# One-hot columns and six tiles of rows of a routing table, built by comparisons with a scalar per partition

## The chip, the cores and the metric

The kernel runs on one core of a Trainium2 chip. The metric is the device time of one execution in microseconds (us), from the first to the last instruction with what lies around them. Three runs of the kernel before gave 1054.81 us as their median (1053.97 to 1056.63).

## What is computed

Two residual blocks follow one another on `x` (8 x 256 tokens of 512 numbers): a cross attention, and a mixture of experts. Only the second matters here:

```python
logits = x2d @ gate_w.T                       # 2048 tokens, 32 experts
rw = softmax(logits)
_, sel = top_k(sigmoid(logits), 4)            # 4 experts per token
w = take_along_axis(rw, sel); w = w / w.sum(-1)
large = sum over e of (silu(x @ Wg[e]) * (x @ Wu[e]) * cw_large[:, e]) @ Wd[e]      # 192 wide
small = the same with 16 shared experts, expert e // 2                               # 128 wide
x = x + large + 0.05 * small
```

The 2048 tokens give 8192 pairs of a token and an expert. The kernel sorts the pairs by expert into slots of 128 rows and computes one expert in each slot.

## The kernel before

There are three stages: `attention`, `route` and `experts`. Each is a block in which the five engines run their own programs and meet at its end.

**Attention** takes about the first 390 us and is not touched.

**Route** (L991 on) works on 16 tiles (`NT`) of 128 tokens, in 4 groups of 4 (`GT`). TensorE makes the logits. VectorE takes the four largest (`largest`), and its `rows(g)` works out the place of each pair within its expert. The low seven bits of the place are the row within a slot; their negative is kept in `rf`, an fp32 tensor with one value for each token of a tile and each of the `K_` = 4 choices. The rest of the place and the first slot of the expert give the slot, `qf`, an fp32 tensor of the same shape. There are `NS` = 96 possible slots.

The table of tokens by row and slot is then a sum of 64 products on TensorE (L1302), four to a tile: a 128 x 128 fp16 matrix `rown[:, t, k, :]`, which in each partition (a token) holds the token's number in the column of its row and 0 elsewhere, times a 128 x 96 fp16 matrix `ohq[:, t, k, :]`, which holds 1 in the column of its slot. For each tile TensorE waits for `rown` (`rown_ready`) and for `ohq` (`ohq_ready`).

`rown` is made in two ways. For tiles 0 to 9 (`COMPARED` = 10) ScalarE makes it alone, in its own `rows(g)`: four activations (L1165) take the distance |iota + rf| into `away`, and a fifth (L1168) turns it into number * relu(1 - distance). For tiles 10 to 15 VectorE compares first: one `tensor_tensor` for a tile (L1413) compares `iota_n` (0, -1, -2, ...; fp16, repeated over the 4 choices by a stride of 0) with `rf` (repeated over the 128 columns) into `ohr`, 4 x 128 fp16 elements to a partition; ScalarE then multiplies it by the token's number (`numbers(t)`, L1149) after its last `rows` and after it has issued the store of the weights (L1204).

VectorE's order in this part is its own program's: `rows(2)`, `rows(3)`, ten small instructions (L1401 to L1410), the six comparisons of `ohr` (L1413), a wait for TensorE's `base_full` (the product at L1295, which waits for ScalarE's last `oh_evac`, L1154), `qf` (L1416), then sixteen comparisons of `ohq` (L1418), one for a tile with 4 x 96 fp16 elements to a partition, then a wait for TensorE's `tab_full` and five instructions (L1422 to L1427) that turn the table into `tok` and `dst`, the lists by which the experts gather and add rows. With `dst` the block ends.

**Experts** (L1430 on) begins when all engines have left the route block. GpSimd gathers 128 rows by `tok` (L1501, L1504), VectorE turns them (L1599), a chain of small transfers issued by ScalarE turns them further (L1545, `xT`), and TensorE computes gate and up (L1636), a transpose (L1645) and down (L1653), for 78 slots one after the other.

Of the kernel before, what the change touches and what calls it, by code (L numbers as in the profile page):

```python
# [5 lines left out]
ALU = mybir.AluOpType  # L6
ACT = mybir.ActivationFunctionType
# [5 lines left out]
F16 = mybir.dt.float16  # L13

P = 128
# [4 lines left out]
NT = NB * TT  # L20
# [942 lines left out]
E_, K_ = 32, 4  # L963
TILE = P
NS = (NT * P * K_) // TILE + E_
# [10 lines left out]
COMPARED = 10  # L976
# [14 lines left out]
def route(nc, gw, gw_loaded, xs, ident, new, xd, out, tabs, wts, W, w_loaded, kept, xd_stored):  # L991
# [5 lines left out]
    with ExitStack() as ctx:  # L997
        sb = lambda n, s, d: ctx.enter_context(nc.sbuf_tensor(n, s, d))
        ps = lambda n, s: ctx.enter_context(nc.psum_tensor(n, s, F32))
        sem = lambda n: ctx.enter_context(nc.semaphore(n))  # L1000
# [20 lines left out]
        iota_r = sb("iota_r", [P, P], F16)  # L1021
        iota_q = sb("iota_q", [P, NS], F16)
        iota_n = sb("iota_n", [P, P], F16)
        ohr = sb("ohr", [P, NT - COMPARED, K_, P], F16)
        none = sb("none", [P, 1], F32)
        number, minus = sb("number", [P, NT], F32), sb("minus", [P, NT], F32)
        away = [sb(f"away{i}", [P, K_, P], F16) for i in range(2)]
# [10 lines left out]
        rf, jf, qf = (sb(n, [P, NT, K_], F32) for n in ("rf", "jf", "qf"))  # L1038
# [5 lines left out]
        rown = sb("rown", [P, NT, K_, P], F16)  # L1044
        ohq = sb("ohq", [P, NT, K_, NS], F16)
# [9 lines left out]
        step = sem("r_step")  # L1055
        var_ready, ln_ready, root_ready, late_ready = sem("r_var"), sem("r_ln_ready"), sem("r_root"), sem("late_ready")
        zeros_ready, zeros_stored, w_ready, w_stored = sem("zeros_ready"), sem("zeros_stored"), sem("w_ready"), sem("w_stored")
        ohr_ready = sem("ohr_ready")
        id4_ready, ohq_ready = sem("id4_ready"), sem("ohq_ready")
        oh_ready, ohT_full, ohT_ready, bsel_ready, base_full = (sem(n) for n in (  # L1060
            "oh_ready", "ohT_full", "ohT_ready", "bsel_ready", "base_full"))
        minus_ready, rf_ready, away_ready, rown_ready = (sem(n) for n in ("minus_ready", "rf_ready", "away_ready",
                                                                         "rown_ready"))
# [8 lines left out]
        def of(g):  # L1072

            return slice(g * GT, (g + 1) * GT)
# [5 lines left out]
        @block.sync  # L1080
        def _(sp):
            for n in range(2):
                load_piece(sp, wts, W, w_loaded, 0, 0, n)
            for t in range(LATE, NT):
                sp.wait_ge(late_ready, t - LATE + 1)
                sp.dma_start(xd[t * P:(t + 1) * P, 0:D], xl[:, t - LATE, :]).then_inc(xd_stored, DMA)
            sp.wait_ge(zeros_ready, 1)
            sp.dma_start(out[NT * P:(NT + 1) * P, :], zeros[:, :]).then_inc(zeros_stored, DMA)
            for p in range(1, NW):
                for n in range(2):  # L1090
                    load_piece(sp, wts, W, w_loaded, 0, p, n)
            for p in range(2):
                sp.wait_ge(kept[p], NT // 2 * DMA)
            sp.wait_ge(xd_stored, NT * DMA)
            sp.wait_ge(zeros_stored, DMA)
            sp.wait_ge(w_stored, DMA)
# [30 lines left out]
        @block.scalar  # L1127
        def _(act):
            def x_evac(t):
                act.wait_ge(xt_full, t + 1)  # L1130
                if t // GT >= 2:
                    act.wait_ge(part_full, t // GT - 1)
                act.copy(xnT[t // GT % 2][:, :, t % GT * P:(t % GT + 1) * P],
                         xt_ps[t % 2][:, :].rearrange("p (c t) -> p c t", c=C)).then_inc(xt_empty, 1)

            def parts_evac(g):
                act.wait_ge(part_full, g + 1)
                if g >= 2:
                    act.wait_ge(lg_full, g - 1)
                act.copy(parts[g % 2][:, :], part_ps[g % 2][:, :]).then_inc(part_ready, 1)  # L1140

            def lg_evac(g):
                act.wait_ge(lg_full, g + 1)
                act.copy(lg[:, of(g), :], lg_ps[:, of(g), :]).then_inc(lg_ready, 1)

            def numbers(t):

                act.wait_ge(ohr_ready, t - COMPARED + 1)
                act.activation(rown[:, t, :, :], ohr[:, t - COMPARED, :, :], ACT.Copy,  # L1149
                               scale=number[:, t:t + 1]).then_inc(rown_ready, 1)  # L1150

            def oh_evac(g):
                act.wait_ge(ohT_full, g + 1)
                act.copy(ohT[:, of(g), :], xt_ps[g % 2][:, :].rearrange("p (t n) -> p t n", t=GT)).then_inc(ohT_ready, 1)  # L1154

            def exponentials(g):
                act.wait_ge(d4_ready, g + 1)
                act.activation(e4[:, of(g), :], d4[:, of(g), :], ACT.Exp).then_inc(e4_ready, 1)

            def rows(g):  # L1160

                act.wait_ge(rf_ready, g + 1)
                for t in range(g * GT, min((g + 1) * GT, COMPARED)):
                    for k in range(K_):
                        m = act.activation(away[t % 2][:, k, :], iota_r[:, :], ACT.Abs, bias=rf[:, t, k:k + 1])  # L1165
                    m.then_inc(away_ready, 1)
                    act.wait_ge(away_ready, t + 1)
                    act.activation(rown[:, t, :, :], away[t % 2][:, :, :], ACT.Relu, bias=number[:, t:t + 1],  # L1168
                                   scale=minus[:, t:t + 1]).then_inc(rown_ready, 1)

            act.preload_act_table_set("natural_log_exp_and_others")
            x_evac(0)
            x_evac(1)
            act.wait_ge(var_ready, 1)
            act.activation(ln[:, LATE:NT], mv[:, LATE:NT, 1], ACT.Ln, bias=eps[:, :]).then_inc(ln_ready, 1)
            act.wait_ge(ln_ready, 1)
            act.activation(root[:, LATE:NT], ln[:, LATE:NT], ACT.Exp, scale=-0.5).then_inc(root_ready, 1)
            for t in range(2, GT + 2):
                x_evac(t)
            for g in range(NG - 1):  # L1180
                parts_evac(g)
                x_evac((g + 1) * GT + 2)
                lg_evac(g)
                x_evac((g + 1) * GT + 3)
                if g < NG - 2:
                    x_evac((g + 2) * GT)
                    x_evac((g + 2) * GT + 1)
                    exponentials(g)
            parts_evac(NG - 1)
            lg_evac(NG - 1)  # L1190
            exponentials(NG - 2)
            act.wait_ge(minus_ready, 1)
            act.wait_ge(iotas, 2)
            oh_evac(0)
            rows(0)
            oh_evac(1)
            oh_evac(2)
            exponentials(NG - 1)
            rows(1)
            oh_evac(NG - 1)  # L1200
            rows(2)

            act.wait_ge(w_ready, NG)
            act.dma_start(xd[:, D:D + E_].rearrange("(t p) e -> p t e", p=P), wrow[:, :, :]).then_inc(w_stored, DMA)  # L1204
            for t in range(COMPARED, NT):
                numbers(t)

        @block.tensor
        def _(pe):
# [84 lines left out]
            for t in range(NT):  # L1294
                m = pe.matmul(lg_ps[:, t, 0:K_], ohT[:, t, :], bsel[:, :], start=True, stop=True)  # L1295
            m.then_inc(base_full, 1)

            for t in range(NT):
                pe.wait_ge(rown_ready, t + 1)
                pe.wait_ge(ohq_ready, t + 1)  # L1300
                for k in range(K_):
                    m = pe.matmul(tab_ps[:, 0:NS], rown[:, t, k, :], ohq[:, t, k, :], start=(t == 0 and k == 0),  # L1302
                                  stop=(t == NT - 1 and k == K_ - 1))
# [3 lines left out]
        def _(dve):  # L1307
# [102 lines left out]
            dve.tensor_scalar(slot_buf[:, 0:NS], slot_e[:, 0:NS], NW - 1, None, ALU.bitwise_and)  # L1410

            for t in range(COMPARED, NT):
                dve.tensor_tensor(ohr[:, t - COMPARED, :, :], iota_n[:, :].unsqueeze(1).broadcast_to([P, K_, P]),  # L1413
                                  rf[:, t, :].unsqueeze(2).broadcast_to([P, K_, P]), ALU.is_equal).then_inc(ohr_ready, 1)
            dve.wait_ge(base_full, 1)
            done(dve.tensor_tensor(qf[:, :, :], lg_ps[:, :, 0:K_], jf[:, :, :], ALU.add))  # L1416
            for t in range(NT):
                dve.tensor_tensor(ohq[:, t, :, :], iota_q[:, :].unsqueeze(1).broadcast_to([P, K_, NS]),  # L1418
                                  qf[:, t, :].unsqueeze(2).broadcast_to([P, K_, NS]), ALU.is_equal).then_inc(ohq_ready, 1)

            dve.wait_ge(tab_full, 1)
            done(dve.tensor_copy(tabf[:, :], tab_ps[:, 0:NS]))  # L1422
# [317 lines left out]
```

## Time and profile before

| | |
|---|---|
| median of three runs | 1054.81 us |
| the profiled execution: its own time | 1054.6 us |
| its span | 1052.9 us |
| TensorE busy | 983.6 us (93%) |
| VectorE busy | 524.5 us (50%) |
| ScalarE busy | 314.0 us (30%) |
| mean granted TensorE clock | 0.968 of full speed |

PE is TensorE's matmuls and PEld its weight loads, DVE is VectorE, ACT ScalarE, POOL GpSimd, SP SyncE. "L1418" is line 1418 of the kernel. Times are us from the first instruction, means of one instruction are in ns. "idle before" is the time that an engine stood still ahead of the instructions of a group, and "<-" names what it waited for. An instruction's duration is longer than the interval from its start to the start of the next on the same engine, because independent instructions overlap.

### The profile page before, as it was taken

How to read it: one execution, taken by the hardware profiler on the slowest of the kernel's cores; microseconds unless marked ns; L12 is line 12 of the kernel's file. 1: busy time of each engine (PE TensorE's matmuls, PEld its weight loads, DVE VectorE, ACT ScalarE, POOL GpSimd, SP SyncE). 2: the span in 40 equal slices, each digit the busy share in tenths (PEclk: the TensorE clock that was granted, in tenths of full speed). 3: DMA queues.
4: the chain of work that ended last, by engine and by line, in shares of the span. 5: the costliest groups of instructions: out<-in, count | busy, mean ns of one | idle time of the engine just before them, and what ended most of it. 6: DMA issues, size and time to landing. Idle time of an engine off the chain costs nothing.

```text
span 1052.9 us, 18703 instructions
## 1 busy us (share of the span) xinstructions
PE 983.6 (93%) x5163; PEld 723.9 (69%) x5164; DVE 524.5 (50%) x1233; ACT 314.0 (30%) x631; POOL 300.2 (29%) x399
## 2 busy tenths in 40 slices
PE   8789999999999987449999999999999999999994
PEld 6556667676665545337787777878777787877872
DVE  5677677777677727923333333333333333333331
ACT  2245465555555536801111111111111111111110
POOL 3012101011120002223443434344343443434432
PEclk9999999999999999569999999999999999999997
DMA  6153234331431019138888998989888899889563
GB/s 215 44 163 77 75 84 102 87 87 58 121 80 51 32 41 354 47 83 201 217 219 199 253 252 213 259 206 256 201 224 213 207 259 244 214 207 252 113 112 71
DMA packets 102603, 168.23 MB, mean 160 GB/s; under 512 B 15520, under 2 KB 65824, under 8 KB 98208
## 3 DMA queue, kind: packets, MB, share of 16 engines
q1 hardware_dynamic: 36624, 103.11, 31.3%
q0 software_dynamic: 17792, 43.30, 22.6%
q10 hardware_dynamic: 48144, 21.25, 7.3%
q8 instruction: 27, 0.44, 0.2%
q14 instruction: 16, 0.13, 0.0%
HBM read 101.29 MB, written 29.36 MB: 124 GB/s over the span
## 4 chain that ended last, share of the span: by engine, by line
PE 55%; DMA 1%; issue 1%; DVEq 0%; DVE 0%; ACTq 0%; POOL 0%; ACT 0%; POOLq 0%
PE y_ps L1653 19%; PE g_ps L1636 17%; PE u_ps L1636 16%; PE at_ps L1645 2%; DMA xg<-xd,gidx 0%; DMA xT<-xb 0%; ACTq L1545 0%; POOL out_x L1518 0%; DVEq L1621 0%; DVE xb L1599 0%; ACT sg L1550 0%; DVEq L1586 0%; ACT yb L1556 0%; DVE aT L1582 0%; DVEq L1622 0%
## 5 line engine op out<-in xcount | busy, mean ns | idle before, releaser
L1653 PE MATMUL y_ps<-W,aT 128*128 x468 | 216.2, 598 | 3.6 <-DVE aT L1582 3.6
L1518 POOL DMA_INDIRECT out_x<-yb,yidx x78 | 125.3, 1606 | 278.4 <-ACT yb L1556 159.7
L1636 PE MATMUL g_ps<-W,xT 128*128 x624 | 192.5, 452 | 12.8 <-DMA xT<-xb 12.8
L519 DVE TENSOR_REDUCE mx<-s 128x2 f32<-128x512 f32 x256 | 163.6, 682 | 59.4 <-PE s L710 58.6
L398 ACT ACTIVATE pt<-stp 128x512 f32<-128x512 f32 x256 | 139.1, 596 | 146.6 <-PE stp L724 145.9
L1636 PE MATMUL u_ps<-W,xT 128*128 x624 | 180.7, 432 | 0.0
L1636 PEld LDWEIGHTS g_ps<-W,xT 128*128 128x128 f32 x624 | 168.3, 311 | 15.2 <-issue 15.1
L1636 PEld LDWEIGHTS u_ps<-W,xT 128*128 128x128 f32 x624 | 171.0, 308 | 0.1
L1653 PEld LDWEIGHTS y_ps<-W,aT 128*128 128x128 f32 x468 | 89.6, 192 | 85.7 <-issue 79.6
L1599 DVE STREAM_TRANSPOSE xb<-xg 128x512 f32<-128x512 f32 x80 | 89.1, 1114 | 102.6 <-DMA xg<-xd,gidx 99.8
L1550 ACT ACTIVATE sg<-g_ps 128x320 f32<-128x320 f32 x78 | 34.2, 438 | 302.4 <-PE u_ps L1636 302.4
L1603 DVE SCALAR_TENSOR_TENSOR a<-u_ps,wt,sg 128x192 f32<-128x192 f32 x78 | 32.6, 418 | 160.8 <-ACT sg L1550 158.9
L1556 ACT COPY yb<-y_ps 128x512 f32<-128x512 f32 x78 | 45.7, 585 | 201.2 <-DMA out_x<-yb,yidx 125.4
L1504 POOL DMA_INDIRECT xg<-xd,gidx x82 | 82.7, 1008 | 65.4 <-POOL gidx L1501 64.7
L710 PE MATMUL s<-kst,qst 96*128 96x256 bf16 x512 | 81.6, 274 | 10.8 <-DVE mx L519 9.9
L1582 DVE COPY aT<-at_ps 128x384 f32<-128x384 f32 x78 | 43.5, 558 | 86.8 <-PE at_ps L1645 81.9
L724 PE MATMUL stp<-qst,kst 98*128 98x256 bf16 x512 | 78.5, 276 | 4.2 <-DMA qst<-nm 4.1
L710 PEld LDWEIGHTS s<-kst,qst 96*128 96x128 bf16 x512 | 43.7, 97 | 51.8 <-DVE mx L519 24.5
L740 PE MATMUL ov<-pt,vx 128*32 128x256 f32 x1024 | 70.3, 393 | 2.0 <-ACT xo L382 2.0
L1501 POOL COPY gidx<-tok 128x1 uint32 (+1 forms) x82 | 60.0, 732 | 28.1 <-POOLq L997 17.2
L724 PEld LDWEIGHTS stp<-qst,kst 98*128 98x128 bf16 x512 | 49.4, 98 | 17.7 <-issue 5.7
L1645 PEld LDWEIGHTS at_ps<-ident,a 128*128 128x128 f32 x234 | 30.2, 140 | 43.7 <-issue 42.0
(203 smaller groups left out, 869.5 us busy)
## 6 DMA issues: line engine op xcount, KB each, us to landing
W<-in_wts SPq DMA_DIRECT2D x32, 1280.0 KB
W<-in_wts SPq DMA_DIRECT2D x32, 768.0 KB
xT<-xb ACTq DMA_DIRECT2D x320, 64.0 KB
qst<-q SPq DMA_DIRECT2D x42, 256.0 KB, 5.0
xs<-in_x SPq DMA_DIRECT2D x8, 512.0 KB, 3.7
ctxT<-in_ctx SPq DMA_DIRECT2D x8, 512.0 KB, 4.2
out_x<-xs SPq DMA_DIRECT2D x16, 256.0 KB, 2.3
kst<-k SPq DMA_DIRECT2D x48, 64.0 KB, 2.3
```

Source lines behind the costliest of these rows:

```text
L398: act.activation(pt[g % 2][:, 2 * (j % 2) + r, :, :], stp[n % STP][:, :, :], ACT.Exp, scale=DH ** -0.5).then_inc(exp_done, 1)
L519: dve.tensor_reduce(mx[j // CH % 2][:, h:2 * G:G], s1[r][:, :, :], AX.X, ALU.max)\
L710: m = pe.matmul(s1[r][:, t, :], qst[b % 2][0:ROWS_QK, head(j, r), t * P:(t + 1) * P], kst[b % 2][0:ROWS_QK, head(j, r) // C, :], start=Tru ...
L724: m = pe.matmul(stp[n % STP][:, t, :], kst[b % 2][0:ROWS_ST, head(j, r) // C, t * P:(t + 1) * P], qst[b % 2][0:ROWS_ST, head(j, r), :], st ...
L740: m = pe.matmul(ov[c * VW:(c + 1) * VW, g % 2, :], vx[b % 2][:, t, g % 2 * C + c, :], pt[(b * G + g) % 2][:, c, t, :], start=(t == 0), sto ...
L1501: pool.tensor_copy(idx[p][:, :], tok[:, bass.ds(s, 1)]).then_inc(idx_ready, 1)
L1504: pool.indirect_dma_start(xg[p][:, :], None, xd[:, :], bass.IndirectOffsetOnAxis(idx[p][:, :], 0))\
L1518: pool.indirect_dma_start(out[:, :], bass.IndirectOffsetOnAxis(yidx[p][:, :], 0), yb[p][:, :], None, compute_op=ALU.add).then_inc(y_added, ...
L1599: dve.transpose(xb[p][:, :].rearrange("p (j r c) -> p j c r", r=Q, c=C), xg[p][:, 0:D]).then_inc(turned, 1)
L1636: m = pe.matmul(ps_[p][:, 0:IW], xT[p][:, :, c], W[:, bass.ds(buf, 1), (2 * c + g) * IW:(2 * c + g + 1) * IW] .rearrange("p a f -> p (a f) ...
L1645: m = pe.transpose(at_ps[:, c, :], a[p][:, c * P:(c + 1) * P], ident[:, :])
L1653: m = pe.matmul(y_ps[:, :], aT[p][:, c, :], W[:, bass.ds(buf, 1), GW + c * D:GW + (c + 1) * D].rearrange("p a d -> p (a d)"), start=(c == ...
```

## The change

The six comparisons of `ohr` and ScalarE's six multiplications go. VectorE makes `rown` of tiles 10 to 15 itself, by 24 `tensor_scalar` instructions, four to a tile: each takes 128 columns of `iota_n`, compares with one column of `rf` (a scalar for each partition, read through a pointer) and multiplies by `number` (a second such scalar). The sixteen comparisons of `ohq` become 64 `tensor_scalar` instructions, four to a tile, each of 96 columns of `iota_q` with one such scalar, a column of `qf`. A semaphore is raised by the last instruction of a tile; `late_rows` takes the place of `rown_ready` for tiles 10 to 15. Nothing else is changed; the buffer `ohr` is dropped.

```diff
@@ route @@
-        ohr = sb("ohr", [P, NT - COMPARED, K_, P], F16)
...
-        ohr_ready = sem("ohr_ready")
+        late_rows = sem("late_rows")
@@ ScalarE @@
-            def numbers(t):
-
-                act.wait_ge(ohr_ready, t - COMPARED + 1)
-                act.activation(rown[:, t, :, :], ohr[:, t - COMPARED, :, :], ACT.Copy,
-                               scale=number[:, t:t + 1]).then_inc(rown_ready, 1)
...
-            for t in range(COMPARED, NT):
-                numbers(t)
@@ TensorE @@
             for t in range(NT):
-                pe.wait_ge(rown_ready, t + 1)
+                if t < COMPARED:
+                    pe.wait_ge(rown_ready, t + 1)
+                else:
+                    pe.wait_ge(late_rows, t - COMPARED + 1)
                 pe.wait_ge(ohq_ready, t + 1)
@@ VectorE @@
             for t in range(COMPARED, NT):
-                dve.tensor_tensor(ohr[:, t - COMPARED, :, :], iota_n[:, :].unsqueeze(1).broadcast_to([P, K_, P]),
-                                  rf[:, t, :].unsqueeze(2).broadcast_to([P, K_, P]), ALU.is_equal).then_inc(ohr_ready, 1)
+                for k in range(K_):
+                    m = dve.tensor_scalar(rown[:, t, k, :], iota_n[:, :], rf[:, t, k:k + 1], number[:, t:t + 1],
+                                          ALU.is_equal, ALU.mult)
+                m.then_inc(late_rows, 1)
             dve.wait_ge(base_full, 1)
             done(dve.tensor_tensor(qf[:, :, :], lg_ps[:, :, 0:K_], jf[:, :, :], ALU.add))
             for t in range(NT):
-                dve.tensor_tensor(ohq[:, t, :, :], iota_q[:, :].unsqueeze(1).broadcast_to([P, K_, NS]),
-                                  qf[:, t, :].unsqueeze(2).broadcast_to([P, K_, NS]), ALU.is_equal).then_inc(ohq_ready, 1)
+                for k in range(K_):
+                    m = dve.tensor_scalar(ohq[:, t, k, :], iota_q[:, :], qf[:, t, k:k + 1], None, ALU.is_equal)
+                m.then_inc(ohq_ready, 1)
```

## Rows read from the trace of the kernel before

**Rows 1.** The page: busy tenths in 40 slices of 26.3 us each.

```profile
PE   8789999999999987449999999999999999999994
DVE  5677677777677727923333333333333333333331
PEclk9999999999999999569999999999999999999997
```

**Rows 2.** Chain of work that ended last, 425 to 470: start, us, what.

```profile
448.68 0.19 POOL gidx L1501
...
456.49 2.92 DMA xT<-xb
...
459.66 4.25 PE g_ps L1636 x8
```

**Rows 3.** Busy time by stretch; behind each engine's (x instructions) PEclk, DMA share, GB/s.

```profile
434.80:438.60 3.80, 0.59 (x16) 0.51 (x16) 3.80 (x8) 3.73 (x9) 0.00 (x0) 0.50 0.01 2
438.60:446.90 8.30, 7.51 (x64) 4.70 (x64) 7.63 (x17) 5.75 (x12) 0.00 (x0) 0.50 0.21 34
...
600.00:800.00 200.00, 200.00 (x684) 157.56 (x683) 72.23 (x163) 28.22 (x55) 81.44 (x109) 1.00 0.89 230
```

**Rows 4.** Timeline of the table's making: start, us, engine, line, what.

```profile
434.81 3.69 DVE L1413 TENSOR_TENSOR ohr<-iota_n,rf 128x512 f16<-128x512 f16 x6
436.73 0.59 PE L1295 MATMUL r_lg<-bsel,ohT 128*128 128x4 bf16 x16 [7.75 <-ACT ohT L1154]
438.42 0.22 DVE L1416 TENSOR_TENSOR qf<-r_lg,jf 128x64 f32<-128x64 f32 x1
438.67 7.59 DVE L1418 TENSOR_TENSOR ohq<-iota_q,qf 128x384 f16<-128x384 f16 x16
439.90 0.81 ACT L1168 ACTIVATE rown<-away,number,minus 128x512 f16<-128x512 f16 x1
440.62 3.77 ACT L1149 ACTIVATE rown<-ohr,number 128x512 f16<-128x512 f16 x6
446.38 0.29 PEld L1302 LDWEIGHTS tab_ps<-ohq,rown 128*128 128x128 f16 x4 [0.17 <-issue]
```

**Rows 5.** Timeline of DVE behind the table, 446.8 to 448.9.

```profile
446.92 0.26 DVE L1422 COPY tabf<-tab_ps 128x96 f32<-128x96 f32 x1 [0.66 <-PE tab_ps L1302]
447.22 0.27 DVE L1424 TENSOR_SCALAR empty<-tabf,none 128x96 f32<-128x96 f32 x1
447.52 0.21 DVE L1425 TENSOR_SCALAR tok<-tabf 128x96 uint32<-128x96 f32 x1
```

**Rows 6.** Groups of DVE instructions: xcount | busy us, mean ns | idle before.

```profile
L1413 DVE TENSOR_TENSOR ohr<-iota_n,rf 128x512 f16<-128x512 f16 x6 | 3.7, 684 | 0.0
L1418 DVE TENSOR_TENSOR ohq<-iota_q,qf 128x384 f16<-128x384 f16 x16 | 7.6, 551 | 0.0
L1377 DVE TENSOR_SCALAR iota_n<-iota_r 128x128 f16<-128x128 f16 x1 | 0.2, 188 | 0.0
L1404 DVE TENSOR_SCALAR more<-cum_i 128x1 int32<-128x1 int32 x1 | 0.2, 154 | 0.0
```

**Rows 7.** Timeline of DVE at 399.7, x5 in a row.

```profile
399.70 2.37 DVE L1372 TENSOR_SCALAR xl<-xs,mv_new,rstd_new 128x512 f32<-128x512 f32 x5
401.99 0.17 DVE L1376 TENSOR_SCALAR minus<-number 128x16 f32<-128x16 f32 x1
```

**Rows 8.** Timeline of DVE, 427.2 to 428.7.

```profile
427.48 0.25 DVE L1393 TENSOR_SCALAR bsel<-kmask,basep 128x4 bf16<-128x4 f32 x1
427.65 0.17 DVE L1394 TENSOR_TENSOR end_x<-cum,ident 32x32 f32<-32x32 f32 x1
...
428.06 0.26 DVE L1396 TENSOR_SCALAR past<-iota_s,end 32x96 bf16<-32x96 f32 x1
428.25 0.15 DVE L1341 TENSOR_REDUCE s<-e 128x4 f32<-128x16 f32 x1
```

**Rows 9.** DMA issues, 395 to 475: engine op xcount, KB each, us to landing.

```profile
xd<-wrow ACTq DMA_DIRECT2D x1, 256.0 KB, 3.3
```

## The prediction

> **What bounds the kernel now.** I read the busy tenths first [rows 1]. TensorE is at 9 tenths nearly everywhere, except in two slices at about 421 to 473 us, the route and the start of the experts. VectorE is at 9 tenths in one slice of the whole span, and it is the same one. So a change to VectorE's comparisons in the route can matter there only. Next the chain that ended last [rows 2]: from 448.68 on it is the gather with its index, the turning transfer, and from 459.66 TensorE alone, slot after slot. In the stretch 600 to 800 TensorE is busy 200.00 of 200.00 us [rows 3], so there is no slack behind the route in which a delay could vanish or a gain be lost: a microsecond at 448 is a microsecond at the end.
>
> Third, the stretches ahead of that point [rows 3]. From 434.8 to 438.6 VectorE is busy 3.80 of 3.80 us, with the six comparisons of `ohr`; from 438.6 to 446.9 it is busy 7.63 of 8.30 us, with `qf` and the sixteen comparisons of `ohq`. GpSimd does nothing in either. TensorE's 64 matmuls run beside `ohq`, but they follow it: the last four weight loads start at 446.38, behind the last comparison's end at 438.67 + 7.59 = 446.26 [rows 4], and VectorE waits 0.66 us for their product, until 446.92 [rows 5]. ScalarE's six multiplications of `ohr` run from 440.62 to 444.39 [rows 4], for tiles 10 to 15, whose `ohq` comes later: they lie under VectorE's work. So the end of the route is VectorE's own queue: `ohr`, `qf`, `ohq`, the wait for TensorE, five small instructions. The question is only whether 24 + 64 `tensor_scalar` take less or more of VectorE's time than 6 + 16 `tensor_tensor`.
>
> **What the removed instructions cost.** L1413 takes 684 ns for 512 elements, L1418 551 for 384 [rows 6]. The difference is 133 ns for 128 elements, 1.04 ns for one: one element in a cycle of 0.96 GHz. What counts in a queue of independent instructions is the interval. The six `ohr` take from 434.81 to 438.42, where `qf` starts: 3.61 us, 0.602 each, that is 0.533 for the elements and 0.069 fixed. The sixteen `ohq` take 7.59 us [rows 4], with an interval of (7.59 - 0.55) / 15 = 0.469, 0.400 and again 0.069.
>
> **What an added instruction costs.** No row shows this form in a queue, so I build its price from three parts.
>
> Elements: L1377, 128 fp16 elements with a constant, takes 188 ns, and L1404, one element, 154 [rows 6]. The difference of 34 ns for 127 elements is four in a cycle. For 128 elements that is 33 ns and for 96 it is 25.
>
> Fixed: 0.069 in the interval as above, the same in both kinds of `tensor_tensor`.
>
> The scalar for each partition: L1372 has two of them. Its five run in a row, 2.37 us with the last at 541 ns by this count: the interval to L1376 included it is (401.99 - 399.70) / 5 = 0.458 [rows 7]. Its 512 fp32 elements would take 0.533 at one in a cycle, which is more than the whole, so they go at two, 0.267. With 0.069 fixed, 0.122 is left, 0.061 for each scalar. L1424 and L1425 say the same in durations: both have 96 fp32 elements, L1424 compares, multiplies and has one such scalar, 0.27 against 0.21 [rows 5], 0.06 more. L1424 also shows that a comparison does not fall to one element a cycle, since that alone would be 0.05 more. A larger value stands in L1393, four elements and one scalar: L1394 starts 0.17 behind it [rows 8], so up to 0.10 for the scalar. From L1396 (96 elements, one scalar) to L1341 it is 0.19 [rows 8].
>
> So one added `ohr` instruction: 0.069 + 2 x 0.061 + 0.033 = 0.224. One added `ohq` instruction: 0.069 + 0.061 + 0.025 = 0.155 by this sum, at least 0.17 if L1393's interval is a floor, and at most L1396's 0.19. I take 0.16, nearest the sum, because L1372 is the only row that shows such instructions behind one another.
>
> **A rule beside it.** The row above gives each such instruction an interval of 0.155 us or more. The Trainium skill (VectorE: DVE Perf Modes, The TRN2 errata) has 58 cycles + elements / mode for an instruction from SBUF to SBUF, with no term for a scalar that is read through a pointer: an estimate of 82 cycles, 0.085 us, for 96 fp16 elements at four a cycle. For the removed L1418 it gives 442 cycles, 0.460, and the trace agrees with 0.469. By it the change would gain some 3 us. The same page's rules for kernel authors say to minimize the number of operations, which speaks against 88 in place of 22.
>
> **The sum.**
> - `ohr`: 24 x 0.224 = 5.38 us in place of 3.61: +1.77. `qf` then starts at 440.2. Its operand from TensorE is there at 436.73 + 0.59 = 437.32 [rows 4], so the wait for it costs nothing, as before.
> - `ohq`: 63 x 0.16 + 0.24 for the last one whole = 10.32 us in place of 7.59: +2.73. With 0.155 it is +2.4, with 0.17 +3.4, with 0.19 +4.6.
> - ScalarE's six multiplications, 3.77 us: nothing gained, they were hidden under `ohq`. Its last `rown` of its own, tile 9, comes at 440.71 [rows 4]; `ohq` of tile 9 would be ready at about 440.5 + 10 x 0.64 = 446.9, so TensorE doesn't wait for ScalarE.
> - TensorE: its four matmuls for a tile fit in 0.47 us now [rows 4], and would have 0.64. The 0.66 us behind the last comparison stays.
> - The end of the block: SyncE also waits for the store of the weights, issued at 439.90 (L1204, right ahead of L1149 in ScalarE's queue, so not moved) and landing 3.3 us later [rows 9], about 443.2: hidden.
> - The granted clock is 0.50 through these stretches [rows 3], the lower level of 1.2 GHz, since TensorE does little; it would be so for longer, but TensorE has nothing on the path until 459.66 but four short matmuls.
>
> Together +1.77 + 2.73 = +4.5 us. The profiled execution took 1054.6 us of its own, 0.2 below the median of 1054.81; from the median the forecast is 1059.3 us. Bounds of this case: +4.1 (0.155) to +5.2 (0.17), +6.4 with 0.19.
>
> What a measurement can tell from no change is 0.3%, 3.2 us, here.
>
> **The rivals.**
> 1. *The scalar costs nothing in a queue*, its read lying under the instruction ahead. Then `ohr` takes 24 x 0.102 = 2.45 us and ends at 437.26; `qf` waits until about 437.4 for TensorE: -1.0. `ohq` takes 63 x 0.094 + 0.18 = 6.1: -1.5. Together -2.5: 1052.3 us, on the other side, though within what can be told; the point from which it decides is 0.11 us for an `ohq` instruction, below which the stage becomes shorter if `ohr` is cheap too. The page's formula would be a little beyond it. Against it stands L1372: five in a row, 0.122 us more each than elements and fixed part. 10%.
> 2. *The faster mode isn't had*: with an fp32 scalar the fp16 elements go at two a cycle. `ohr` 24 x 0.257 = 6.18 (+2.57), `ohq` 63 x 0.18 + 0.27 = 11.6 (+4.0): +6.6, 1061.4 us. For it: all rows with a pointer have fp32 elements, so none shows four a cycle. 8%. At one a cycle it would be 24 x 0.324 (+4.2) and 63 x 0.230 + 0.32 (+7.2): 1066.2 us; L1372 and L1424 speak against. 4%.
> 3. *0.10 for each scalar*, as L1393 has it: `ohr` 24 x 0.302 = 7.25 (+3.6), `ohq` 63 x 0.194 + 0.28 = 12.5 (+4.9): +8.5, 1063.3 us. Against it: L1372's two scalars cost 0.122 together, and L1393's scalar had been written by the instruction just ahead. 9%.
> 4. *The delay is taken up further on*, so that the time is the same. Only the start of the experts has room, TensorE's idle time until 459.66, and it begins with the gather, which needs `tok`. 4%.
>
> **How the numbers follow.** The forecast has 65%: 1059.3 us, by its bounds 1058.9 to 1061.2. The range leaves out rivals 1 and 4 and the one-a-cycle case, 18%: 1056.8 to 1063.8 us. Faster by over 0.3% (below 1051.65): the far side of rival 1, 3%. Within 0.3%: the rest of rival 1, rival 4, and a forecast whose `ohq` comes out under 0.14: 16%. Slower by over 0.3%: 81%.
>
> **What the profile after would show.** L1149 gone from ScalarE; 24 instructions into `rown` on VectorE of about 310 ns (0.154 + 0.122 + 0.033), 0.22 apart, and 64 into `ohq` of about 240 ns, 0.16 apart; `qf` at 440.2, the last `ohq` ending at 450.8, `tabf` at 451.4, the first gather's index at 453.2, TensorE's first gate matmul at 464.2, and every slot from there as long as before. Durations near 190 for `ohq` mean rival 1, 265 rival 2, 280 rival 3. The prediction is wrong if the intervals in these two runs of instructions aren't what the sum says, or if the interval between `tabf` and the first gate matmul is not 12.7 us as now.

## The result and the profile after

The changed kernel takes 1058.76 us (median of 22 runs), the kernel before, run beside it, 1054.33 us (22 runs). The ratio is 1.0039, with a 95% interval of 1.0024 to 1.0054: slower by 0.39%, 4.1 us (2.5 to 5.7). The two medians themselves lie 4.4 us apart, well inside that interval. The measured time is inside the range of the prediction and on the side it gave 81%. It fits the forecast of +4.5 us closer than a measurement with this interval can tell, so how near the two came is in part luck.

The timeline of the changed kernel where the table is made (start, us, engine, line, what), to be laid beside [rows 4] and [rows 5]. Line numbers have moved: L1408 writes `rown`, L1415 writes `ohq`, L1419 is `tabf`.

```profile
432.81 5.43 DVE L1408 TENSOR_SCALAR rown<-iota_n,rf,number 128x128 f16<-128x128 f16 x24
434.76 0.59 PE L1286 MATMUL r_lg<-bsel,ohT 128*128 128x4 bf16 x16 [7.76 <-ACT ohT L1147]
437.93 0.81 ACT L1161 ACTIVATE rown<-away,number,minus 128x512 f16<-128x512 f16 x1
438.14 0.24 DVE L1412 TENSOR_TENSOR qf<-r_lg,jf 128x64 f32<-128x64 f32 x1
438.42 2.72 DVE L1415 TENSOR_SCALAR ohq<-iota_q,qf 128x96 f16<-128x96 f16 x17
...
440.89 7.49 DVE L1415 TENSOR_SCALAR ohq<-iota_q,qf 128x96 f16<-128x96 f16 x48
...
449.04 0.26 DVE L1419 COPY tabf<-tab_ps 128x96 f32<-128x96 f32 x1 [0.66 <-PE tab_ps L1296]
```

Two lengths are to be read. From the first late `rown` to `qf` it is 438.14 - 432.81 = 5.33 us, where the six comparisons took 3.61. From the first `ohq` to the end of the last it is 440.89 + 7.49 - 438.42 = 9.96 us, where they took 7.59. Whole, from the first of these instructions to `tabf`: 16.23 us in place of 446.92 - 434.81 = 12.11, +4.12 us, which lies in the interval of the measured difference. ScalarE's L1149 is gone, and the engine has nothing to compute from 438.7 on; that gives nothing back.

The groups of the same stretch (mean ns of one) and TensorE's waits in it:

```profile
L1415 DVE TENSOR_SCALAR ohq<-iota_q,qf 128x96 f16<-128x96 f16 x64 | 10.0, 245 | 0.0
L1296 PE MATMUL tab_ps<-ohq,rown 128*128 128x96 f16 x64 | 7.6, 269 | 6.0 <-DVE ohq L1415 3.9
L1408 DVE TENSOR_SCALAR rown<-iota_n,rf,number 128x128 f16<-128x128 f16 x24 | 5.4, 322 | 0.0
```

VectorE has no idle time ahead of either group. The chain that ended last shows what lies behind:

```profile
450.80 0.20 POOL gidx L1498
...
461.77 4.65 PE g_ps L1633 x8
```

From `tabf` to the first gate matmul it is 461.77 - 449.04 = 12.73 us, and was 459.66 - 446.92 = 12.74. Behind it TensorE is full, as in [rows 3] (busy by stretch: PE, PEld, DVE, ACT, POOL, then the granted clock, DMA share, GB/s):

```profile
600.00:800.00 200.00, 199.98 (x680) 156.48 (x680) 72.65 (x166) 28.10 (x55) 82.41 (x110) 1.00 0.89 231
```

The points in time that the prediction gave (`qf` at 440.2, `tabf` at 451.4) are off by 2.0 us although the lengths are right: this execution reached the stage 2.0 us sooner, 432.81 against 434.81, in work that the change doesn't touch. The span in the profile therefore grew by 2.4 us only, and the medians are what tells the difference. This is taken up in the last section.

### The profile page after: what moved, and what is told of

It reads as the page before. It is cut to its first block, busy times and chain, and to the rows that moved or that the text cites. A ratio compares the mean times of both kernels' runs of the same rounds, so it can differ in the third digit from the quotient of the medians.

```text
span 1055.3 us, 18763 instructions
## 1 busy us (share of the span) xinstructions
PE 981.2 (93%) x5163; PEld 722.5 (68%) x5164; DVE 529.8 (50%) x1299; ACT 310.2 (29%) x625; POOL 300.9 (29%) x399
## 4 chain that ended last, share of the span: by engine, by line
PE 54%; DMA 1%; issue 1%; DVEq 0%; DVE 0%; ACTq 0%; POOL 0%; ACT 0%; SPq 0%; POOLq 0%
PE y_ps L1650 19%; PE g_ps L1633 17%; PE u_ps L1633 16%; PE at_ps L1642 2%; DMA xg<-xd,gidx 0%; DMA xT<-xb 0%; ACTq L1542 0%; POOL out_x L1515 0%; DVEq L1618 0%; DVE xb L1596 0%; ACT sg L1547 0%; DVEq L1583 0%; ACT yb L1553 0%; DVE aT L1579 0%; DVEq L1619 0%
## 5 line engine op out<-in xcount | busy, mean ns | idle before, releaser
L1633 PE MATMUL g_ps<-W,xT 128*128 x624 | 192.6, 452 | 13.0 <-DMA xT<-xb 12.8
```

The source lines that it names most:

```text
L1633: m = pe.matmul(ps_[p][:, 0:IW], xT[p][:, :, c], W[:, bass.ds(buf, 1), (2 * c + g) * IW:(2 * c + g + 1) * IW] .rearrange("p a f -> p (a f) ...
```

## The experiments

**The slots alone.** The kernel before with the edit of `ohq` only.

```diff
             for t in range(NT):
-                dve.tensor_tensor(ohq[:, t, :, :], iota_q[:, :].unsqueeze(1).broadcast_to([P, K_, NS]), ...
+                for k in range(K_):
+                    m = dve.tensor_scalar(ohq[:, t, k, :], iota_q[:, :], qf[:, t, k:k + 1], None, ALU.is_equal)
+                m.then_inc(ohq_ready, 1)
```

> Only the comparisons of ohq by a scalar per partition (64 in place of 16); ohr and ScalarE's multiplications as before. My account: the sixteen tiles of ohq take 9.95 us from the first to the end of the last, in place of 7.59, so +2.4 us in all, 0.2%: from the start of ohr to tabf 14.5 us in place of 12.11. Rival (the slower table lets ScalarE's own work come on the path, or the delay is taken up further on): TensorE waits for rown, or the distance from tabf to the first gate matmul is not 12.7 us.

Measured: ratio 1.0019 (1.0002 to 1.0036), 1057.16 us. The timeline of this run:

```profile
437.62 3.70 DVE L1413 TENSOR_TENSOR ohr<-iota_n,rf 128x512 f16<-128x512 f16 x6
...
441.49 9.96 DVE L1419 TENSOR_SCALAR ohq<-iota_q,qf 128x96 f16<-128x96 f16 x64
443.47 3.77 ACT L1149 ACTIVATE rown<-ohr,number 128x512 f16<-128x512 f16 x6
...
447.25 0.29 PEld L1302 LDWEIGHTS tab_ps<-ohq,rown 128*128 128x128 f16 x4 [0.32 <-ACT rown L1149]
...
452.11 0.26 DVE L1423 COPY tabf<-tab_ps 128x96 f32<-128x96 f32 x1 [0.66 <-PE tab_ps L1302]
```

From the first `ohr` to `tabf` 14.49 us, expected 14.5, +2.4. From `tabf` to the first gate matmul (464.86) 12.75 us. The profile puts six waits of TensorE's weight loads, 1.9 us in all, down to ScalarE's late rows (L1149). That can't be the cause: these waits lie between 443.8 and 447.3, ahead of tiles 3 to 8, which use none of the late rows, and the last of those rows was done at 447.24 (443.47 + 3.77), before tile 10 began. TensorE waited for `ohq`, tile by tile, 0.62 us apart, and `tabf` waits the same 0.66 us. The rival is out.

**The rows alone.** The changed kernel with its `ohq` put back to sixteen `tensor_tensor`, so that only the late rows are by `tensor_scalar`.

```diff
             for t in range(COMPARED, NT):
-                dve.tensor_tensor(ohr[:, t - COMPARED, :, :], iota_n[...], rf[...], ALU.is_equal).then_inc(ohr_ready, 1)
+                for k in range(K_):
+                    m = dve.tensor_scalar(rown[:, t, k, :], iota_n[:, :], rf[:, t, k:k + 1], number[:, t:t + 1],
+                                          ALU.is_equal, ALU.mult)
+                m.then_inc(late_rows, 1)
```

> Only the rows of the last six tiles by VectorE alone (24 in place of 6, no multiplications on ScalarE); ohq as before. My account: the 24 take 5.33 us in place of 3.61, so +1.7 us: 13.85 us from the first of them to tabf. ScalarE's freed 3.77 us give nothing back. Rival (ScalarE's multiplications held TensorE up in the kernel before): less than +1.7, with TensorE's table matmuls ending closer behind the last ohq.

Measured: ratio 1.0005 (0.9991 to 1.0020), 1054.68 us. The time can't tell it from no change, nor from the expected 1.0016. The timeline can:

```profile
436.07 5.44 DVE L1408 TENSOR_SCALAR rown<-iota_n,rf,number 128x128 f16<-128x128 f16 x24
...
441.41 0.23 DVE L1412 TENSOR_TENSOR qf<-r_lg,jf 128x64 f32<-128x64 f32 x1
441.67 7.59 DVE L1414 TENSOR_TENSOR ohq<-iota_q,qf 128x384 f16<-128x384 f16 x16
...
449.92 0.26 DVE L1418 COPY tabf<-tab_ps 128x96 f32<-128x96 f32 x1 [0.66 <-PE tab_ps L1296]
```

It is 13.85 us from the first late row to `tabf`, +1.74. That is the number expected, but the expectation took its 5.33 us from the changed kernel's trace; new is that the halves add up and that ScalarE gives nothing back: `tabf` waits 0.66 us for TensorE as before, so ScalarE's multiplications had not held anything up. The two halves, +2.38 and +1.74, add up to the +4.12 of the whole.

**The price of a scalar.** These lengths fit the prediction's sum, but one alone fits others too: 0.155 us could be 0.069 fixed, 0.061 for the scalar and 96 elements at four a cycle, or the same fixed part, 0.036 for the scalar and elements at two a cycle. By the second reading an instruction of the late rows would take 0.069 + 2 x 0.036 + 0.067 = 0.208 us where 0.222 was measured, which speaks against it, but by 0.014 us and with a fixed part that is itself inferred. So the parts were measured by themselves, in queues of 12 behind the end of the route in the changed kernel.

```diff
             done(dve.tensor_scalar(dst[:, :], far[:, :], 1.0, None, ALU.subtract))
+            for i in range(12):
+                m = dve.tensor_scalar(junk[:, i, 0:NS], iota_q[:, :], 3.0, None, ALU.is_equal)
+            done(m)
+            for i in range(12):
+                m = dve.tensor_scalar(junk[:, i, 0:NS], iota_q[:, :], qf[:, i, 0:1], None, ALU.is_equal)
+            done(m)
...
+            for i in range(12):
+                done(dve.tensor_scalar(fresh[:, i:i + 1], number[:, i:i + 1], 1.0, None, ALU.mult))
+                dve.tensor_scalar(junk[:, i, 0:4], iota_q[:, 0:4], fresh[:, i:i + 1], None, ALU.is_equal)
+                done(dve.tensor_scalar(junk[:, i, 8:12], iota_q[:, 0:4], 3.0, None, ALU.is_equal))
```

> The changed kernel, and behind its last instruction in the route seven queues of 12 independent instructions each on VectorE into buffers that nothing reads: fp16, 96 elements with a constant; with one scalar per partition; with two; 4 elements with one; 96 fp32 elements with one; a tensor_tensor of 384 fp16 elements whose innermost dimension is the four choices, contiguous in all three operands; and a pair in which the scalar has been written by the instruction ahead. My account (0.069 fixed, 0.061 for a scalar, four fp16 elements a cycle, two fp32): intervals 0.094, 0.155, 0.216, 0.131, 0.180, 0.27 us. Rival that the faster mode is lost beside a scalar (two fp16 a cycle, so a scalar costs 0.035): 0.094, 0.155, 0.19, 0.106, 0.155. Rival that a floor of 0.15 to 0.17 stands for any instruction with a scalar, whatever its size: the third and fourth are both near 0.155 to 0.17. The pair: 0.17 from the instruction with the fresh scalar to the next, if L1393's row means that a scalar just written is dearer; 0.131 if it doesn't.

The timeline of that run. The interval is (length - duration of one) / 11, in the last queue the mean from the start of the instruction with the scalar to the start of the next. "One" is the median duration.

```profile
449.95 0.26 DVE L1424 COPY tabf<-tab_ps 128x96 f32<-128x96 f32 x1 [0.66 <-PE tab_ps L1301]
...
451.83 1.22 DVE L1433 TENSOR_SCALAR junk<-iota_q 128x96 f16<-128x96 f16 x12
453.08 1.95 DVE L1436 TENSOR_SCALAR junk<-iota_q,qf 128x96 f16<-128x96 f16 x12
455.06 2.67 DVE L1439 TENSOR_SCALAR junk<-iota_q,qf,number 128x96 f16<-128x96 f16 x12
457.77 1.66 DVE L1442 TENSOR_SCALAR junk<-iota_q,qf 128x4 f16<-128x4 f16 x12
459.46 2.24 DVE L1445 TENSOR_SCALAR junk<-iota_s,qf 128x96 f32<-128x96 f32 x12
461.74 3.31 DVE L1448 TENSOR_TENSOR junk<-iota_qk,q 128x384 f16<-128x384 f16 x12
...
465.28 0.23 DVE L1453 TENSOR_SCALAR junk<-iota_q,fresh 128x4 f16<-128x4 f16 x1
465.41 0.17 DVE L1454 TENSOR_SCALAR junk<-iota_q 128x4 f16<-128x4 f16 x1
...
482.87 4.65 PE L1663 MATMUL g_ps<-W,xT 128*128 x8 [32.96 <-DMA xT<-xb]
```

| queue | one, ns | interval, us | expected |
|---|---|---|---|
| 96 fp16, a constant | 186 | 0.094 | 0.094 |
| 96 fp16, one scalar | 244 | 0.155 | 0.155 |
| 96 fp16, two scalars | 303 | 0.215 | 0.216 |
| 4 fp16, one scalar | 224 | 0.131 | 0.131 |
| 96 fp32, one scalar | 261 | 0.180 | 0.180 |
| 384 fp16, `tensor_tensor`, choices innermost | 354 | 0.269 | 0.27 |
| 4 fp16, the scalar just written | 229 | 0.136 | 0.131 or 0.17 |

Each scalar adds 0.061, the first and the second alike. 92 elements more add 0.024 us beside a scalar, which is four a cycle: the faster mode is kept. And a small instruction with a scalar goes at 0.131, so there is no floor at 0.155 to 0.17. Both rivals are out. A scalar that has just been written costs 0.005 us more at most, so the 0.17 behind L1393 [rows 8] has another cause, which none of these runs shows.

This run also shows how much of a delay in this place arrives at the end: the queues, with two copies ahead of them, take from 451.20 to 471.32, 20.1 us. From `tabf` to the first gate matmul it is 482.87 - 449.95 = 32.92 us, 20.2 more than in the changed kernel. The program ran once, in 1079.17 us, 20.4 more than the changed kernel's median; runs of that kernel lie up to 9 us apart, so this last agreement is worth less than the one in the trace.

**Two a cycle for the `tensor_tensor`.** The queues say that a `tensor_tensor` can have what the change sought, if its operands allow it: fp16 throughout, with the same innermost dimension of step 1, which here are the four choices. The scalars are kept in fp16, GpSimd writes the counting columns four times over at the start, where it is idle, and TensorE and ScalarE read with a stride of four. VectorE then has time to spare and ScalarE has not, so `COMPARED` goes to 8.

```diff
-COMPARED = 10
+COMPARED = 8
...
-        ohr = sb("ohr", [P, NT - COMPARED, K_, P], F16)
+        ohr = sb("ohr", [P, NT - COMPARED, P, K_], F16)
...
-        ohq = sb("ohq", [P, NT, K_, NS], F16)
+        ohq = sb("ohq", [P, NT, NS, K_], F16)
...
-            pool.iota(iota_q[:, :], [[1, NS]], 0, 0, allow_small_or_imprecise_dtypes=True)
+            pool.iota(iota_qk[:, :, :], [[1, NS], [0, K_]], 0, 0, allow_small_or_imprecise_dtypes=True)
+            pool.iota(iota_rk[:, :, :], [[1, P], [0, K_]], 0, 0, allow_small_or_imprecise_dtypes=True)
...
+            dve.tensor_copy(r16[:, COMPARED:NT, :], ri[:, COMPARED:NT, :])
...
-                dve.tensor_tensor(ohq[:, t, :, :], iota_q[:, :].unsqueeze(1).broadcast_to([P, K_, NS]),
-                                  qf[:, t, :].unsqueeze(2).broadcast_to([P, K_, NS]), ALU.is_equal).then_inc(ohq_ready, 1)
+                dve.tensor_tensor(ohq[:, t, :, :], iota_qk[:, :, :],
+                                  q16[:, t:t + 1, :].broadcast_to([P, NS, K_]), ALU.is_equal).then_inc(ohq_ready, 1)
```

> The kernel before with tensor_tensor kept, but fp16 operands whose innermost dimension is the four choices, contiguous in both inputs and the output (the scalars in fp16, the counting columns repeated four times by GpSimd at the start), and COMPARED 8 in place of 10, so that VectorE and ScalarE share the rows otherwise. My account: two elements a cycle in place of one, 0.336 us for a tile of ohr (eight tiles, 2.7 us in place of 3.6) and 0.27 for a tile of ohq (4.3 in place of 7.6); then TensorE's matmuls at the low clock or ScalarE's eight multiplications (until about 441.8 on the clock of the rows of before) end last, tabf at about 443.6 in place of 446.92: -3.3 us. Rival (the stride of 0 in the second input keeps the one element a cycle): no gain, durations 550 and 684 ns as before. Rival (the strided reads by TensorE and ScalarE cost more): TensorE's matmuls longer than 280 ns apiece or ScalarE's multiplication longer than 707.

Measured: ratio 0.9967 (0.9952 to 0.9983), 1050.63 us, faster than both kernels. Its timeline:

```profile
433.15 2.77 DVE L1415 TENSOR_TENSOR ohr<-iota_rk,r 128x512 f16<-128x512 f16 x8
...
434.84 5.30 ACT L1151 ACTIVATE rown<-ohr,number 128x512 f16<-128x512 f16 x8
...
436.09 4.39 DVE L1420 TENSOR_TENSOR ohq<-iota_qk,q 128x384 f16<-128x384 f16 x16
436.60 5.71 PE L1304 MATMUL tab_ps<-ohq,rown 128*128 128x96 f16 x64 [1.01 <-DVE ohq L1420]
442.34 0.26 DVE L1424 COPY tabf<-tab_ps 128x96 f32<-128x96 f32 x1 [1.86 <-PE tab_ps L1304]
```

9.19 us from the first `ohr` to `tabf`, in place of 12.11: -2.9, expected -3.3 by the times in the rows of before (a cast of the rows to fp16, 0.08 us, lies ahead of this length). The stride of 0 sits in the middle dimension now and doesn't keep it from going at two elements a cycle. The fp32 operand and the stride of 0 in the innermost dimension went together here, so which of the two had held it at one a cycle isn't shown. VectorE is done 1.86 us before `tabf`: TensorE ends last, with 64 matmuls in 5.71 us. ScalarE's multiplication takes 759 ns here in place of 707, and 731 in the next run, which reads with the same stride; so the stride is not the whole of it. A TensorE matmul is recorded with 265 ns in place of 280 (medians), but what counts is the interval, which is taken up in the last section.

The same with `COMPARED` left at 10:

> As the run with the four choices innermost, but COMPARED left at 10. My account: VectorE's work shrinks as there (six tiles of ohr 2.1 us, sixteen of ohq 4.4), but ScalarE ends its own rows of tile 9 only 5.9 us behind the first ohr and needs six multiplications of 0.66 us then, so its last rown comes 9.9 us behind the first ohr, and tabf at about 10.5, in place of 9.19 there and 12.11 in the kernel before: about -1.6 us, with TensorE waiting for ScalarE's rown. Rival (ScalarE's multiplications are hidden as in the kernel before, so COMPARED makes no difference): tabf 9.2 us behind the first ohr.

Measured: ratio 0.9978 (0.9960 to 0.9995), 1052.03 us.

```profile
436.83 2.10 DVE L1415 TENSOR_TENSOR ohr<-iota_rk,r 128x512 f16<-128x512 f16 x6
...
439.56 4.39 DVE L1420 TENSOR_TENSOR ohq<-iota_qk,q 128x384 f16<-128x384 f16 x16
...
442.57 3.93 ACT L1151 ACTIVATE rown<-ohr,number 128x512 f16<-128x512 f16 x6
447.11 0.26 DVE L1424 COPY tabf<-tab_ps 128x96 f32<-128x96 f32 x1 [3.16 <-PE tab_ps L1304]
```

10.28 us, expected 10.5. VectorE is as fast as in the run before this one and waits 3.16 us at the end. ScalarE's late rows, free under the slow `ohq`, now end at 446.50 and bound the stage. Work that is hidden in one version is a price in the next.

Last, the operand of `qf` made earlier, and `ohr` and `ohq` in turn, on top of `COMPARED` 8:

```diff
@@ ScalarE, rows(g) @@
                 for t in range(g * GT, min((g + 1) * GT, COMPARED)):
+                    if t == GT + 1:
+                        oh_evac(NG - 1)
...
             rows(1)
-            oh_evac(NG - 1)
-            rows(2)
@@ VectorE @@
-            for t in range(COMPARED, NT):
-                dve.tensor_tensor(ohr[:, t - COMPARED, :, :], iota_rk[:, :, :], ...)
...
+            late = COMPARED
             for t in range(NT):
                 dve.tensor_tensor(ohq[:, t, :, :], ...)
+                if t >= 1 and late < NT:
+                    dve.tensor_tensor(ohr[:, late - COMPARED, :, :], iota_rk[:, :, :], ...)
+                    late += 1
```

> The run with COMPARED 8 and the four choices innermost; ScalarE also turns its last oh_evac (the operand of the wait for base_full) ahead of tile 5, and VectorE makes qf and the ohq of tiles 0 and 1 first and then ohr and ohq in turn, so that TensorE's table matmuls start earlier. My account: in that run TensorE ended last, 64 matmuls of 0.087 us, 1.86 us behind VectorE; now VectorE's queue of 7.1 us ends last, and tabf comes about 8.0 us behind slot_buf's end in place of 9.19: -1.1 us more, 0.1%, too little for the clock but to be seen in the trace. Rival (ScalarE's order sets it): TensorE waits for rown of the late tiles, no gain.

Measured: ratio 0.9958 (0.9943 to 0.9974), 1050.24 us. From the start of the table's work on VectorE to `tabf` it is 443.52 - 435.03 = 8.49 us in place of 9.19: -0.7 where -1.1 was expected. The lines on which this rests:

```profile
436.75 5.27 ACT L1151 ACTIVATE rown<-ohr,number 128x512 f16<-128x512 f16 x8
439.78 0.35 DVE L1418 TENSOR_TENSOR ohq<-iota_qk,q 128x384 f16<-128x384 f16 x1
440.25 0.32 PEld L1304 LDWEIGHTS tab_ps<-ohq,rown 128*128 128x128 f16 x4 [0.29 <-ACT rown L1151]
440.39 1.97 DVE L1418 TENSOR_TENSOR ohq<-iota_qk,q 128x384 f16<-128x384 f16 x7
440.86 2.40 PEld L1304 LDWEIGHTS tab_ps<-ohq,rown 128*128 128x128 f16 x28 [0.29 <-ACT rown L1151]
443.52 0.26 DVE L1426 COPY tabf<-tab_ps 128x96 f32<-128x96 f32 x1 [1.16 <-PE tab_ps L1304]
```

The profile puts 1.7 us of TensorE's waits, in six places, down to ScalarE's late rows, as the rival has it. But each of these rows was done before the `ohq` of its tile: the first at 437.5 with its `ohq` at 440.13, the last at 442.02 with its `ohq` at 442.36. TensorE starts a tile 0.12 us behind the end of its `ohq` (440.13 and 440.25) and so goes at the pace of VectorE's pairs, one tile in 0.61 us. Then VectorE's last seven `ohq` come 0.27 us apart and TensorE, at 0.34 us a tile, falls behind: `tabf` comes 1.16 us behind the last `ohq` and not 0.66, and this 0.5 us is what was missing (0.25 for `qf`, 7.08 for the queue, 0.66 would be 8.0). The rival is out; the order of VectorE's work lets TensorE wait at first and gives it more than it can take at the end. The intervals of the two ratios overlap; only the trace tells the two versions apart.

## Why the prediction was right

- *VectorE's queue ends the stage, and what is behind it passes a delay on whole.* Right: idle time 0.0 ahead of both groups, `tabf` behind TensorE by 0.66 us in both kernels, 12.73 us from there to the first gate matmul, and 20.1 us of added queue arriving there as 20.2. From that matmul to the last instruction the eight profiled executions took 593.2 to 594.8 us, in no order of the stage's length. This scatter of 1.5 us is one reason why the times and the lengths in the trace don't agree to the tenth.
- *An added `ohr` instruction: 0.224.* Measured 5.33 / 24 = 0.222. The term was +1.77 and came out as +1.72 to +1.74. One such instruction lasts 322 ns, where about 310 was given, which changes nothing in a queue.
- *An added `ohq` instruction: 0.16.* This is the one term that was mis-sized. The sum of fixed part, scalar and elements said 0.155, and the prediction went up to 0.16 because of L1393's row. It is 0.155, so the term is +2.37 in place of +2.73. That is nearly the whole difference between the forecast of +4.5 and the +4.12 of the trace; the measured time can't resolve it.
- *Rival 1, a scalar that costs nothing in a queue:* out, 0.155 against 0.094 with a constant. The 58 cycles and no term for a scalar of the Trainium skill (VectorE: DVE Perf Modes, The TRN2 errata) give an estimate of 0.085 us for an instruction whose interval is 0.155 here; with a constant it is 0.094. The point from which this rival was said to decide, 0.11 us, comes out of its own terms as 0.12 (0.094 + 2.65 / 111).
- *Rival 2, the slower mode:* out, by the queue of 4 elements beside that of 96.
- *Rival 3, 0.10 for each scalar:* out; also when the scalar has just been written.
- *Rival 4, a delay taken up further on:* out. From `tabf` to the first gate matmul it is 12.6 to 12.8 us in all versions but the one with the queues, whose extra 20.2 us lie there.
- *Nothing gained on ScalarE:* right, shown by the rows alone (13.85 us, the price of the 24 instructions and no more off it). The same six multiplications become the bound when `ohq` is made quicker.
- *The granted clock is 0.50, "since TensorE does little".* The level is right, the reason is not read from the rows: from 438.6 to 446.9 TensorE is recorded as busy 7.51 of 8.30 us at 0.50 [rows 3]. Nothing in the sum hangs on it.

## What to carry to other kernels

A short VectorE instruction is mostly its fixed part (0.069 us here, against 0.025 for 96 elements): four elements a cycle save 0.3 us on 384 elements, but cutting one instruction into four adds three fixed parts, and each scalar read through a pointer adds nearly as much again, 0.061. Take both from the intervals of instructions that stand behind one another in the trace, not from durations, before splitting anything. And if a `tensor_tensor` goes at one element a cycle, with an fp32 operand that is repeated along the innermost dimension, look first for an order of the dimensions that gives all operands a contiguous innermost one in a 16-bit type: here that took 0.2 us off each instruction without adding one in the loop.

## What was not expected of the hardware

**The start of the route.** A part of the route that the change doesn't touch has two lengths. From the start of `xl` (L1372 before) to the start of the late rows it is 35.1 us in the kernel before (434.81 - 399.70), 35.2 with the rows alone (436.07 - 400.92) and 35.2 in the version with `COMPARED` 10 (436.83 - 401.61), but 34.0 in the changed kernel (432.81 - 398.83), 34.1 with `COMPARED` 8 (433.15 - 399.09), 34.1 in the last version (435.03 - 400.97) and also 34.0 with the slots alone (437.62 - 403.65). In the kernel before, TensorE spends its sixteen transposes there like this (timeline of PE, a queue of 16, then the next operation):

```profile
398.20 3.56 PE L1217 MATMUL r_xt<-ident,xs 128*128 128x128 f32 x16 [0.83 <-ACT r_xnT L1133]
...
401.69 1.16 PE L1226 MATMUL part_ps<-r_xnT,gw 128*32 128x512 f32 x8
```

and in the changed kernel like this:

```profile
397.32 1.15 PE L1208 MATMUL r_xt<-ident,xs 128*128 128x128 f32 x8 [0.83 <-ACT r_xnT L1132]
...
398.81 1.06 PE L1208 MATMUL r_xt<-ident,xs 128*128 128x128 f32 x8 [0.34 <-ACT r_xnT L1132]
...
399.81 1.07 PE L1217 MATMUL part_ps<-r_xnT,gw 128*32 128x512 f32 x8
```

From the first of these transposes to `part_ps` it is 3.49 us there and 2.49 here. What differs is TensorE's granted clock, the third number from the end (a stretch of the kernel before, then one of the changed kernel):

```profile
398.70:401.80 3.10, 3.10 (x18) 2.41 (x20) 2.60 (x8) 2.10 (x6) 0.00 (x0) 0.50 0.92 345
```

```profile
397.30:400.80 3.50, 3.13 (x24) 1.84 (x24) 2.47 (x8) 2.90 (x7) 0.25 (x2) 1.00 0.89 319
```

At 0.50, the level of 1.2 GHz, these transposes start 0.213 us apart, and at 1.00, that of 2.4 GHz, 0.109. The three executions with the longer route (the kernel before, the rows alone, `COMPARED` 10) all have 0.50 to 0.51 in this stretch, and the five with the shorter one 1.00 (the fifth is the one with the queues, 433.71 - 399.73 = 34.0). Why the clock fell in three of them isn't shown: what TensorE did just before is the same in both, eight transposes, 0.83 us idle, then the next. It isn't the change, since kernels with and without it have either length. But this microsecond is as large as a quarter of the effect that was to be measured, and the start of the route itself moves by up to 4.8 us from one profiled execution to another (`xl` at 398.83 to 403.65), which is why the lengths within the stage were compared here and not points in time.

**TensorE's pace in the table.** In the version with `COMPARED` 8 TensorE ended last, at 0.086 us for one matmul of 96 columns ((5.71 - 0.265) / 63). Its granted clock is 0.71 in that stretch, because it rose from one level to the other in the middle of it, when TensorE had been busy without a gap since 436.60:

```profile
437.00:438.00 1.00, 1.00 (x15) 1.00 (x13) 1.00 (x5) 1.00 (x2) 0.00 (x0) 0.50 0.00 0
...
441.00:442.00 1.00, 1.00 (x15) 1.00 (x13) 0.00 (x0) 0.00 (x0) 0.00 (x0) 1.00 0.00 0
```

As many matmuls and weight loads fall into a microsecond at 0.50 as at 1.00, so the clock doesn't set this interval. The stride of four may have a share in it: in the kernel before, whose matmuls read `ohq` without a stride, the fourth matmul of a tile starts 0.20 us behind the first, and in the last version, where TensorE also takes its tiles one at a time at 0.50, it starts 0.24 us behind (starts in the trace). Whether the weight loads (5.51 us busy of 6.20) set the rest was not tried.
